# A group-gated mixture of experts at the end of a network: every expert for every token, or tokens sorted by group

## The reference

```python
flat = (flat - mu) * rsqrt(var + LN_EPS) * ln_scale + ln_bias
h_shared = _swiglu(flat @ shared_in_w.T)                      # 256 hidden features, gate a and value b
out_shared = h_shared @ shared_out_w.T + shared_out_b
g_idx = argmax(flat @ group_gate_w.T + group_bias)            # one of 2 groups
e_sel = logits of the 4 experts of that group + their bias
e_probs = softmax(e_sel); topv, topi = top_k(e_probs, 2)
topv = topv / (topv.sum(-1, keepdims=True) + 1e-08)
disp = g_idx * 4 + topi
h_expert = _swiglu(flat @ expert_in_w.T)                      # one hidden layer for all 8 experts
comb, cnt = topv and 1.0 put at disp, 0 elsewhere
routed = cnt @ expert_out_bias
for e in range(8):
    routed = routed + comb[:, e:e + 1] * (h_expert @ expert_out_weight[e].T)
return out_shared + routed                                    # added to the residual h
```

## Time and profile before

| | us |
|---|---|
| runs: median (lowest to highest of 3) | 1778.42 (1775.73 to 1779.34) |
| profiled execution | 1775.86 |
| its span | 1773.9 |
| PE busy over the span | 1388.5 (78%) |
| DVE busy | 1134.5 (64%) |
| POOL busy | 800.8 (45%) |
| ACT busy | 677.5 (38%) |

### The profile page before, as it was taken

How to read it: one execution, slowest core, us unless ns; L and a number is a source line. 1 busy time by engine, 2 the same in 40 slices (tenths; PEclk the granted TensorE clock), 3 DMA queues, 4 the chain that set the end, 5 groups by cost and what they waited for, 6 DMA issues and landing times. The chain is left out here.

```text
span 1773.9 us, 27554 instructions
## 1 busy us (share of the span) xinstructions
PE 1388.5 (78%) x9068; PEld 992.5 (56%) x9068; DVE 1134.5 (64%) x1837; ACT 677.5 (38%) x1150; POOL 800.8 (45%) x833
## 2 busy tenths in 40 slices
PE   5679999999873332876727848888998699999998
PEld 3567777777542221765625623333334478887877
DVE  2755555555367782211114888888885889888998
ACT  3234444444443321322203548787875311111111
POOL 1455445444320034888865237777743333232331
PEclk9889999999985565999867969999999899999999
DMA  4070000000001032544443000000001000000000
GB/s 168 1 289 15 0 0 0 0 0 0 0 1 26 1 102 64 100 78 86 78 106 128 1 2 2 1 0 0 0 1 40 1 9 13 13 13 13 9 13 17
DMA packets 56803, 61.75 MB, mean 35 GB/s; under 512 B 15507, under 2 KB 46577, under 8 KB 55425
## 3 DMA queue, kind: packets, MB, share of 16 engines
q1 hardware_dynamic: 40835, 49.69, 8.6%
q0 software_dynamic: 13888, 10.24, 4.2%
q10 hardware_dynamic: 2016, 1.00, 0.2%
HBM read 36.49 MB, written 25.59 MB: 35 GB/s over the span
## 5 line engine op out<-in xcount | busy, mean ns | idle before, releaser
L1946 PE MATMUL at_slot<-at_qm,at_ks 128*128 128x512 bf16 (+1 forms) x640 | 160.3, 384 | 19.5 <-DVE at_clip L2151 10.2
L502 PE MATMUL ga_kv<-ga_kern,ga_v 128*128 128x274 f32 x512 | 133.5, 403 | 13.5 <-ACT ga_kern L591 12.6
L2667 DVE TENSOR_REDUCE mx_routed<-mx_weighted 128x128 f32<-128x1024 f32 x69 | 138.1, 2001 | 2.4
L2625 POOL TENSOR_TENSOR mx_h_E<-mx_hid_E,mx_h_E 128x768 fp32r<-128x768 f32 x23 | 43.5, 1890 | 188.8 <-DVE mx_h_E L2657 188.8
L84 PE MATMUL mx_e<-ff_expert_out_high,mx_h_E 128*128 128x512 f32 x276 | 112.3, 407 | 10.7 <-DVE mx_weighted L2664 10.7
L2030 ACT ACTIVATE at_clip<-at_slot,at_four 128x1024 bf16<-128x1024 f32 (+1 forms) x96 | 106.9, 1113 | 32.1 <-PE at_slot L1946 30.3
L1429 POOL DMA_INDIRECT moe_sums<-ex_y,slot_sums x69 | 108.4, 1570 | 22.4 <-issue 20.3
L2151 DVE TENSOR_SCALAR at_clip<-at_slot 128x1024 bf16<-128x1024 f32 (+1 forms) x96 | 116.1, 1218 | 3.1 <-PE at_slot L1946 2.8
L502 PEld LDWEIGHTS ga_kv<-ga_kern,ga_v 128*128 128x128 f32 x512 | 92.2, 189 | 37.8 <-ACT ga_kern L591 16.8
L85 PE MATMUL mx_e<-ff_expert_out_low,mx_h_E 128*128 128x512 f32 x276 | 109.6, 397 | 0.0
L653 POOL TENSOR_TENSOR ga_rot<-ga_by_cos,ga_by_sin 128x274 f32<-128x274 f32 x64 | 48.6, 759 | 134.9 <-DVE ga_by_sin L697 134.9
(11 more groups left out here) (457 smaller groups left out, 3835.9 us busy)
## 6 DMA issues: line engine op xcount, KB each, us to landing
moe_sums<-ga_zeros SPq DMA_DIRECT2D x8, 1152.0 KB, 13.4
ar_rows<-moe_sums SPq DMA_DIRECT2D x34, 256.0 KB, 3.9
ex_down<-in_down SPq DMA_DIRECT2D x32, 192.0 KB, 2.5
token_rows<-ct_rows SPq DMA_DIRECT2D x17, 256.0 KB, 2.4
out_h<-H SPq DMA_DIRECT2D x22, 192.0 KB, 1.9
H<-in_text SPq DMA_DIRECT2D x1, 4096.0 KB, 21.4
patches<-in_patches SPq DMA_DIRECT2D x1, 1728.0 KB, 8.2
ga_sin<-in_sin SPq DMA_DIRECT2D x1, 1644.0 KB, 7.9
```

The source lines that it names most:

```text
L502: last = nc.tensor.matmul(kv[:, e, 0:HALF], v[p][:, mt + 2 * side, e * P:(e + 1) * P], kern[(p + g) % 2][:, side, :], start=mt == 0 and si ...
L1946: last = nc.tensor.matmul(to[r0:r0 + r, g % 2, :].rearrange("p (s n) -> p s n", s=2), ks[m][:, t * P:t * P + r], qm[m][:, 2 * g:2 * g + 2, ...
L2667: nc.vector.tensor_reduce(R[p][t][:], weighted[:].rearrange("p e d -> p d e"), AX.X, ALU.add).then_inc(reduced, 1)
```

## The change

`mix_experts` is rewritten. Each token now meets only the four experts of its own group, and to that end the tokens are sorted by group in DRAM.

- Sorting. While `route` runs, PE transposes all 69 tiles of `F` in 18 groups of up to four (`stage_turn`, four groups ahead of the rank), and ACT copies them to `stage`, rows of 133 floats: the token, its four shares, its number. `rank` gives each token its place by three small matmuls: group 0 from the front of a DRAM list, group 1 from its back. POOL scatters each tile into the list by an indirect DMA. The list (70 tiles, 4.8 MB) has been filled beforehand, on SP's queue in `last_norm`, with a row that goes nowhere (`blank`).
- Shared part. The 23 chunks of 384 tokens now hold the shared expert, the bias and the residual alone; the projection runs in two halves of 128 hidden features (`project(c, f)`). The sum is transposed back to token rows, which SP stores to `out`, now tokens first.
- Sorted part. After shared chunk 19 SP starts to load sorted tiles, four at a time. For 17 chunks of four tiles and one of two, PE projects in two halves, and `experts` does six matmuls of 512 columns a tile, with the half of `expert_out` chosen by a register from the count of group 0. ACT does the activation, the casts of the high parts and the product with the first expert's share (`weigh_first`); DVE adds the other three in three dependent multiply-adds and makes the low parts; POOL adds each finished tile to the rows of `out` by an indirect DMA that accumulates.

The loops are written out, without `Fori`. The semaphores of the earlier expert stage (`run_experts`) are allocated another way.

```diff
--- before.py
+++ after.py
+GT = 4
+GCH = GT * P
+GTILES = -(-(NT + P - 1) // P)
+GROW = P + 5
+BEYOND_BITS = 14
+BEYOND = 1 << BEYOND_BITS
...
+def last_norm(nc, k, x, H, F, GL, high, low, grouped_d):
...
             sp.dma_start(gates[:, 0:10], x["gates"]).then_inc(gates_in, 16)
+            sp.dma_start(grouped_d, x["blank"]).then_inc(blanked, 16)
...
-def mix_experts(nc, k, H, F, GL, high, low, out):
+def mix_experts(nc, k, x, H, F, GL, high, low, grouped_d, out):
...
+        silu = sb("silu", [P, 2, GCH])
+        hid = sb("hid", [P, 2, GCH])
+        LOADS, RING = 4, 6
+        tiles = [F[:, p * GT * GROW:(p + 1) * GT * GROW].rearrange("p (t d) -> p t d", d=GROW) for p in range(LOADS)]
+        R = [F[:, LOADS * GT * GROW + p * P:LOADS * GT * GROW + (p + 1) * P] for p in range(RING)]
+        LOAD_AFTER = CHUNKS - 4
...
+            for c in range(CHUNKS):
+                sp.wait_ge(rows_out, c + 1)
...
+                if c == LOAD_AFTER:
+                    sp.wait_ge(grouped, 1)
+                    for early in range(LOADS):
+                        load(early)
+            for c in range(LOADS, len(CHUNKS2)):
+                load(c)
...
+            def stage_turn(g):
+                t, n = FGROUPS[g]
+                if g >= 2:
+                    pe.wait_ge(staged, g - 1)
+                for i in range(n):
+                    last = nc.tensor.transpose(t_ps[g % 2][:, i * P:(i + 1) * P], F[:, (t + i) * P:(t + i + 1) * P], k["ident"][:])
+                last.then_inc(staged_ps, 1)
...
+            def project2(c, f):
+                n = CHUNKS2[c][1] * P
+                pe.wait_ge(f_low2, c + 1)
...
+                    pe.wait_ge(hidden2, 2 * c - 1 + f)
+                for ps, at in ((a_ps, 0), (b_ps, 2)):
+                    cols = slice((at + f) * P, (at + f + 1) * P)
+                    last = split_matmul(nc, ps[:, f, 0:n], (high["expert_in"][:, cols], low["expert_in"][:, cols]),
+                                        [part[:, 0:n] for part in f_parts[c % 2]], True, True)
+                last.then_inc(projected2, 1)
+
+            def experts(c, i, first_count):
+                j = CHUNKS2[c][0] + i
...
+                    pe.wait_ge(weighed, j - 1)
+                at = (((P * j + BEYOND - first_count) >> BEYOND_BITS) & 1) * 512
...
+                for f in range(2):
+                    if i == 0:
+                        pe.wait_ge(h_low2, 2 * c + 1 + f)
+                    cols = bass.ds(at, 512)
+                    last = split_matmul(nc, e_ps[j % 2][:], [part[:, f, tokens] for part in h[c % 2]],
+                                        (high["expert_out"][:, f, cols], low["expert_out"][:, f, cols]), f == 0, f == 1)
...
+            for c in range(CHUNKS):
+                if c + 1 < CHUNKS:
+                    project(c + 1, 0)
+                    if c > 0:
+                        turn_rows(c - 1)
+                    project(c + 1, 1)
+                    turn_cnt(c + 1)
+                    finish(c)
...
+            for c, (t, n) in enumerate(CHUNKS2):
+                if c < LAST2:
+                    project2(c + 1, 0)
+                if c + 2 <= LAST2:
+                    turn(c + 2)
+                for i in range(n):
+                    experts(c, i, first_count)
+                    if i == min(1, n - 1) and c < LAST2:
+                        project2(c + 1, 1)
...
+            def hide_high(c, f):
+                act.wait_ge(hidden, 2 * c + 1 + f)
+                if c >= 2:
+                    act.wait_ge(y_done, c - 1)
+                nc.scalar.activation(h[c % 2][0][:, f, 0:CH], hid[:, f, 0:CH], ACT.Copy).then_inc(h_high, 1)
...
+            def weigh_first(c, i):
+                j = CHUNKS2[c][0] + i
+                act.wait_ge(expert_done, j + 1)
+                if j >= RING:
+                    act.wait_ge(sent[j % RING], 16 * (j // RING))
+                nc.scalar.activation(R[j % RING], e_ps[j % 2][:, 0:P], ACT.Copy, scale=tiles[c % LOADS][:, i, P:P + 1]).then_inc(first_done, 1)
...
+            for t in range(TILES):
+                if t % 4 == 0:
+                    pool.wait_ge(staged, t // 4 + 1)
+                nc.gpsimd.indirect_dma_start(out=grouped_d, out_offset=bass.IndirectOffsetOnAxis(ap=place_i[:, t:t + 1], axis=0),
+                                             in_=stage[:, t, :], in_offset=None, bounds_check=GTILES * P - 1,
+                                             oob_is_err=False).then_inc(placed, 16)
...
+            for j in range(GTILES):
+                pool.wait_ge(weighed, j + 1)
+                ids = tiles[j // GT % LOADS][:, j % GT, GROW - 1:GROW].bitcast(I32)
+                nc.gpsimd.indirect_dma_start(out=out, out_offset=bass.IndirectOffsetOnAxis(ap=ids, axis=0),
+                                             in_=R[j % RING], in_offset=None, bounds_check=NT - 1, oob_is_err=False,
+                                             compute_op=ALU.add).then_inc(sent[j % RING], 16)
...
+            def weigh(c, i):
...
+                dve.wait_ge(first_done, j + 1)
+                for e in range(1, 4):
+                    if e > 1:
+                        dve.wait_ge(acc, 2 * j + e - 1)
+                    nc.vector.scalar_tensor_tensor(r, part(e), share(e), r, ALU.mult, ALU.add).then_inc(acc if e < 3 else weighed, 1)
```

More of the change, by code:

```diff
@@ L2500, in mix_experts @@
         gt = COLS["gate_b"][0]
[L2502 to L2513, removed]
+        earlier, upper = order[:, 0:P], order[0:TILES, P:P + TILES]
@@ L2521, in _, with load @@
[L2521 to L2523 removed]
+            def load(c):
+                t, n = CHUNKS2[c]
+                if c >= LOADS:
+                    t0, n0 = CHUNKS2[c - LOADS]
+                    for j in range(t0, t0 + n0):
+                        sp.wait_ge(sent[j % RING], 16 * (j // RING) + 16)
+                sp.dma_start(tiles[c % LOADS][:, 0:n, :],
+                             grouped_d[t * P:(t + n) * P, :].rearrange("(t p) d -> p t d", p=P)).then_inc(loaded[c % LOADS], 16)
@@ new lines, in turn_cnt, with finish @@
+            def turn_cnt(c):
+                if c == 0:
+                    pe.wait_ge(counted, 3)
+                    pe.wait_ge(staged, len(FGROUPS))
+                else:
+                    pe.wait_ge(cnt_out, c)
+                for t in range(CT):
+                    last = nc.tensor.transpose(t_ps[0][0:NEX + 1, t * P:(t + 1) * P], cnt[:, CT * c + t, :], k["ident"][:])
+                last.then_inc(cnt_ps, 1)
+            def finish(c):
+                pe.wait_ge(h_low, 2 * c + 2)
+                pe.wait_ge(placed_at if c < 2 else added, 1 if c < 2 else c - 1)
+                for f in range(2):
+                    split_matmul(nc, e_ps[c % 2][:, 0:CH], (high["shared_out"][:, f, :], low["shared_out"][:, f, :]),
+                                 [part[:, f, 0:CH] for part in h[c % 2]], f == 0, False)
+                pe.wait_ge(cnt_out, c + 1)
+                nc.tensor.matmul(e_ps[c % 2][:, 0:CH], high["out_bias"][:], cnt_t[:], start=False, stop=False)
+                nc.tensor.matmul(e_ps[c % 2][:, 0:CH], low["out_bias"][:], cnt_t[:], start=False, stop=True).then_inc(y_done, 1)
@@ L2849, in _arrays @@
     a["owner"] = np.stack([~late, late], 1).astype(f)
+    token = np.arange(NTP).reshape(TILES, P).T
+    real = token < NT
+    front = np.where(real, token, 1 << 20)
+    back = np.where(real, GTILES * P - 1 - token, 0)
+    above = np.zeros((P, TILES))
+    above[:TILES] = np.arange(TILES)[:, None] < np.arange(TILES)[None]
+    a["order"] = np.concatenate([lane[:, None] < lane[None], above, front, back, token, np.ones((P, 1))], 1).astype(f)
+    blank = np.zeros((GTILES * P, GROW), f)
+    blank.view(np.int32)[:, GROW - 1] = NOWHERE
+    a["blank"] = blank
     a["headmask"] = (lane[:, None] // HD == np.arange(HEADS)[None]).astype(f)
```

459 lines of the change are left out of this document (284 added, 175 removed).

## The result

The changed kernel takes 1696.4 us (median, 1694.06 to 1700.57) against 1778.17 for the one before (four executions, one more than in the table of before): a ratio of 0.9544, with an interval of 0.9522 to 0.9567. Forecast were 1717 and a range of 1686 to 1750. The profiled execution took 1694.06 us with a span of 1692.3, where the sum of the prediction came to 1714.5.

A forecast was written before the change was run, and what follows sets the result against it. PE (48.61 of 50 us busy) and DVE (45.31) were taken to bound the kernel. 1420 + 112 + 5 + 7.5 + 163 + 7 = 1714.5 us of span, 1716.5 with 1.96 around it; predicted 1717, range 1686 to 1750.

The forecast's parts named there:

- rival 1: Shared and sorted parts: PE sets the pace of both, the engines' rings overlapping better; span 1684 us, chance 0.16.
- What the change removes: Last stage: four experts a token instead of eight, no DVE reductions; PE's bill before was 343 us.
- A: Routing and staging: first hidden values at about 1420 us, bounds 1414 and 1423, with 1.0 us a staging group.
- The rings, not PE, set B: Shared part: DVE and ACT take 5.1 us a chunk in turn, above PE's floor of 4.40 us.
- B: Shared expert alone, 23 chunks: 22 x 5.1 = 112 us, plus 5 for first chunks and last chunk.
- C: Sorted part, 70 tiles with four experts: DVE's order gives 9.3 us a chunk, 163 us; PE's bound 8.77.
- The load ring: Sorted part: four chunks in the ring; reloading takes 17.4 to 18.3 us against the 18.6 of two chunks.
- rival 2: Sorted part: slower landings make loads set the pace, 10.8 us a chunk, 26 more, 1743 us; chance 0.13.
- The scatter: POOL's 69 indirect DMAs of 1.28 us, 88 us from 1411.5, done near 1503, hidden by the shared part.
- rival 3: Shared and sorted parts: DVE subtractions wait for POOL's indirect DMAs, 20 and 19 us, 1756 us; chance 0.07.
- rival 4: Shared and sorted parts: granted clock stays at 1.2 GHz because PE waits too often, 1942 us; chance 0.05.
- Prices of single operations: Shared and sorted parts: lengths priced for single DVE, ACT and POOL operations, such as 0.55 us for a 384-column DVE add.

The follow-up runs named there:

- p1: Changed kernel with both projections leaving out the product of the weights' high part with the tokens' low part: 1688.82 us, ratio 0.9505.
- u2: Changed kernel with the casts of the hidden halves moved back from ACT to DVE in both parts: 1692.00 us, ratio 0.9511.
- p2: p1 with five chunks of loaded tiles instead of four and eight sums instead of six: 1681.89 us, ratio 0.9458.
- i3: Changed kernel with five chunks of loaded tiles instead of four and eight sums instead of six, all products kept: 1693.91 us, ratio 0.9528.
- u3: Changed kernel with the two halves of the hidden layer made together again in both parts: 1764.44 us, ratio 0.993.
- l3: Changed kernel with three chunks of loaded tiles in the ring instead of four: 1852.91 us, ratio 1.0418.
- i5_all: Changed kernel with one bias matmul, row transposes behind both projection halves, five loads, shared part's hidden casts on DVE: 1688.25 us, ratio 0.9502.

## Why the prediction was right, and where its sizes were not

The time fell in the range, but 1717 was 21 us too long, and 1696 lies outside the likeliest stretch of 1700 to 1735. It lies nearer to rival 1 (a span of 1684, where 1692.3 was measured), which had a chance of 0.16. The range held because it took that rival in; the pace of both parts was not set as forecast.

- **What the change removes** was right: eight experts became four, DVE's reductions went, and the earlier trace rows have no counterpart after. PE's bill by its paces fell from 343 us to 23 x 4.57 + 17.5 x 8.8 = 259, so by 84, and the span fell by 81.6. What writing the loops out is worth by itself was not tried.
- **A** was over-sized by 7.2 us: staging went at 0.67 us a group, not 1.0, and its last copy was done at 1410.9, where 1417 was forecast.
- **"The rings, not PE, set B"** is the step that failed. PE's floor was 4.57 us, not 4.40: more matmuls than in the earlier trace rows stand behind a transpose or a bias matmul, where the next start comes 0.26 to 0.28 us later in place of 0.17. So `finish` takes 1.78 for 1.68, the projection in two halves 1.16 and 1.14 for 2.17, and the two groups of transposes 0.25 each for 0.31 and 0.24:

```profile
1464.62 0.49 PE L2594 MATMUL mx_t<-ident_sb,mx_cnt 128*9 128x128 f32 x3
1464.87 0.42 PE L91 MATMUL mx_e<-mx_h,ff_shared_out_high 128*128 128x384 f32 x1
1465.13 0.34 PE L92 MATMUL mx_e<-mx_h,ff_shared_out_high 128*128 128x384 f32 x1
...
1466.65 0.44 PE L91 MATMUL mx_a<-mx_f,ff_shared_in_high 128*128 128x384 f32 x1
...
1467.81 0.49 PE L2612 MATMUL mx_t<-ident_sb,H 128*128 128x128 f32 x3
```

  The ring of DVE and ACT measured 4.44 where PE was relieved (p1), not 5.1, and PE's floor 4.57 where the ring was (u2). The changed kernel is slower than either, 4.74 in its steady stretch, with PE waiting for DVE's add in every second chunk or so; that PE and ring hold one another up by turns fits this, but no run takes it apart further. In the sum, B lies halfway: 109.4 us, where rival 1 had 102 and the forecast 117.
- **The chain in C** was over-sized: 9.3 forecast, about 8.3 once PE and the loads were out of its way (p2). PE set the pace at 8.7 (i3, means over the part), as rival 1 had it with 8.8, and the waits for loads made 8.86 of it.
- **B's chain was over-sized for one reason**, shown in ACT's rows and in the turn of p1 above: passes were added by listed length, though the next one on the same engine starts some 0.1 us earlier, and handoffs of 0.1 were added where about 0.04 came. For C the same is likely, but was not added up.
- **The load ring** (rival 2) has 17.4 to 18.3 us against two chunks. That figure held: it bound a little with four loads (2.8 us of waits in 100, rival 2's own sign), and with three it took 17.9 us a chunk. The terms given for it do not add up to it, for "two chunks of work" alone would be 18.6; with one chunk, 9.3, and the landings of 3.9 and 3.4, they come to 16.6 without transposes and scatter-add. The landings that rival 2 assumed, 5 and 6 us, did not come: 3.3 and 3.1 in the profile after.
- **The scatter** ran from 1410.7 to its last start at 1502.7, near the forecast (done near 1503), since it began earlier and went at 1.35 us each in the mean, not 1.28. The first load of sorted tiles went out at 1513.0, so none waited for it.
- **The port** (rival 3) did not decide: beside POOL's indirect DMAs, busy 46.42 of 60 us, the token subtraction took at most 0.62 us. Its price was also counted short, with two subtractions a chunk in C, where DVE's order has three.

```profile
L2831 DVE TENSOR_TENSOR mx_f<-ff_tokens,mx_f x23: 546/557/621, 1394.5 to 1510.4; 128x384 fp32r<-128x384 f32 x23
```

- **The clock** (rival 4) stayed at 1.00 wherever PE was kept full, and fell only where an experiment made PE wait (0.87 in u3, 0.76 in the windows of l3). In p1's shared part PE waited about 0.4 us in every chunk and the clock stayed at 1.00. What would make it fall without waits was not tried.
- **Prices of single operations** were right to 0.02 us for 0.55, 0.57 and 0.35 on DVE and 0.48 and 0.53 on ACT. Between POOL's scatter-adds lie 1.85 us (1.89 forecast), and ACT's first product took 0.35 to 0.37 (about 0.3 forecast).

## What to carry to other kernels

Add a chain on one engine by the distance between starts, which a timeline of the kernel before shows, and not by listed lengths; the error here was 0.1 us an instruction and turned the forecast of the bound round. When limits lie within 5% of one another (here, by the means, PE 8.7, loads 8.7, DVE 8.3), relieving one gives little: less PE work alone took 2.8 us off the sorted part and longer rings alone 2.2 to 2.7, but both together took 9.4. Splitting a product in halves paid here where a bank's reader is queued behind it, not where PE has other work to do.

## What the runs showed of the hardware

The cast of a hidden half on DVE, one shape, took 0.36 us or 0.48 to 0.63 within one trace of i5_all:

```profile
L2845 DVE CAST mx_h<-mx_hid x46: 359/528/634, 1416.3 to 1514.6; 128x384 fp32r<-128x384 f32 x46
```

The trace shows what went with it, which is how far POOL was in an indirect DMA of the scatter when the cast began:

```profile
1442.46 0.99 POOL L2816 DMA_INDIRECT by_group<-mx_stage,mx_place_i  x1 [0.30 <-issue]
1442.96 0.36 DVE L2845 CAST mx_h<-mx_hid 128x384 fp32r<-128x384 f32 x1
...
1451.21 0.97 POOL L2816 DMA_INDIRECT by_group<-mx_stage,mx_place_i  x1 [0.30 <-issue]
1451.74 0.63 DVE L2845 CAST mx_h<-mx_hid 128x384 fp32r<-128x384 f32 x1
...
1439.21 1.32 POOL L2816 DMA_INDIRECT by_group<-mx_stage,mx_place_i  x1 [0.30 <-issue]
1440.18 0.53 DVE L2845 CAST mx_h<-mx_hid 128x384 fp32r<-128x384 f32 x1
```

All 11 casts that began up to 0.50 us after the start of such a DMA took 0.36 us. All 19 that began 0.53 to 0.69 after it took 0.48 to 0.63. The ten that began 0.97 or 0.98 after it took 0.53 or 0.54, and the DMA beside them took 1.31 or 1.32, not 0.97. The other six took 0.36. In u2, seven casts began 0.96 to 0.98 us after a DMA, with the same 0.53 and 1.31 to 1.33. So a cast and the end of an indirect DMA go longer where they meet; what in the chip does it, no run tests. The subtractions of the changed kernel, of the same 384 columns, took 0.55 to 0.62 beside the same DMAs.
